# Copying maxima in fewer steps, and preparing the first feed-forward tile beside the end of attention

## What is computed

```
xn  = layernorm(x) * gamma + beta
q, k, v = split(xn @ w_qkv.T)                 # 16 heads of 16
att = softmax(causal(q k^T / 4)) v
x1  = layernorm(x + att)                      # no scale, no shift
h   = silu(x1 w1 * s1) * (x1 w2 * s2)         # 256 -> 1024
h   = gelu(h h1 * s1h); h = gelu(h h2 * s2h)  # 1024 -> 1024, twice
out = layernorm(x1 + h w3 * s3)
```

## Time and profile before

| | us |
|---|---|
| median of 3 launches | 2369.13 (2368.23 to 2370.77) |
| profiled launch, its time | 2370.69 |
| profiled launch, first to last instruction (span) | 2369.0 |
| mean granted TensorE clock, share of 2.4 GHz | 0.987 |

### The profile page before, as it was taken

One profiled execution on the slowest core, in us unless ns is written; L12 is line 12 of the kernel. 1 busy time (PEld: TensorE's weight loads), 2 busy tenths in 40 slices (PEclk: granted clock), 3 DMA queues, 4 the chain that ended last, 5 costly groups with the idle time before them and its releaser, 6 DMA issues. The chain is left out here.

```text
span 2369.0 us, 40425 instructions
## 1 busy us (share of the span) xinstructions
PE 2313.3 (98%) x15360; PEld 1402.8 (59%) x15360; DVE 1737.8 (73%) x3745; ACT 1634.4 (69%) x3221; POOL 204.5 (9%) x266
## 2 busy tenths in 40 slices
PE   5999999999999999999999999999899999999998
PEld 3555554555555455555555555554488888888887
DVE  6889988888889897888879888996335545544543
ACT  2677887788999887888988898999623323332332
POOL 2211100111000101100010211001000000000000
PEclk7999999999999999999999999999899999999999
DMA  4100001100000110000020000205400000000000
GB/s 120 33 23 14 19 19 36 39 19 19 19 11 10 48 28 19 19 19 19 1 50 23 19 19 19 72 2 196 145 1 10 1 9 10 10 1 9 10 1 19
DMA packets 40533, 68.60 MB, mean 29 GB/s; under 512 B 9872, under 2 KB 19984, under 8 KB 38928
## 3 DMA queue, kind: packets, MB, share of 16 engines
q1 hardware_dynamic: 36672, 54.45, 8.4%
q0 software_dynamic: 3664, 11.53, 1.5%
HBM read 28.20 MB, written 4.19 MB: 14 GB/s over the span
## 5 line engine op out<-in xcount | busy, mean ns | idle before, releaser
L620 ACT ACTIVATE PR<-bank 128x512 f32<-128x512 f32 (+3 forms) x2304 | 1110.7, 574 | 61.3 <-PE bank L869 59.1
L696 DVE TENSOR_REDUCE pm<-bank 128x1 f32<-128x512 f32 x1397 | 901.6, 682 | 160.8 <-PE bank L844 145.0
L883 PE MATMUL bank<-PR,V 128*17 128x512 f32 (+3 forms) x4608 | 561.1, 564 | 1.9 <-ACT PR L620 1.2
L1231 PE MATMUL bank<-e_hid,e_h_sb 128*128 128x512 f32 x2048 | 478.1, 395 | 0.0
L864 PE MATMUL bank<-MR,ones 64*128 64x512 f32 (+3 forms) x2304 | 463.4, 390 | 2.2 <-ACT MR L611 0.7
L1231 PEld LDWEIGHTS bank<-e_hid,e_h_sb 128*128 128x128 f32 x2048 | 384.8, 188 | 92.0
L1049 ACT ACTIVATE e_tmp<-bank,e_s_sb 128x512 f32<-128x512 f32 x128 | 88.3, 690 | 342.1 <-PE bank L1231 341.8
L691 DVE TENSOR_REDUCE pm<-mx_sb 128x1 f32<-128x512 f32 x395 | 267.6, 678 | 30.4 <-ACT mx_sb L605 30.3
L864 PEld LDWEIGHTS bank<-MR,ones 64*128 64x128 f32 x2304 | 235.1, 185 | 80.5 <-ACT PR L620 28.9
L605 ACT ACTIVATE mx_sb<-bank 128x512 f32<-128x512 f32 x395 | 238.4, 603 | 45.6 <-PE bank L844 42.1
L699 DVE CUSTOM_DVE_ANT_0 bank<-bank,below 128x384 f32<-128x384 f32 (+3 forms) x512 | 235.7, 520 | 21.3 <-PE bank L844 20.1
(11 more groups left out here) (102 smaller groups left out, 1721.9 us busy)
## 6 DMA issues: line engine op xcount, KB each, us to landing
xnT<-in_h_dram SPq DMA_DIRECT2D x8, 1024.0 KB, 5.7
e_h_sb<-in_h_dram POOLq DMA_DIRECT2D x2, 4096.0 KB, 21.1
KA<-qk_hi SPq DMA_DIRECT2D x96, 64.0 KB, 2.2
KA<-qk_lo SPq DMA_DIRECT2D x96, 64.0 KB, 2.2
QX<-qk_hi SPq DMA_DIRECT2D x80, 64.0 KB, 2.3
QX<-qk_lo SPq DMA_DIRECT2D x80, 64.0 KB, 2.3
xres<-in_x_dram SPq DMA_DIRECT2D x8, 512.0 KB, 8.2
out_dram<-e_y SPq DMA_DIRECT2D x7, 512.0 KB, 2.9
```

Source lines behind the costliest of these rows:

```text
L620: act.activation(PR[:, s % NPB, h, off:QB], ring_bank("score", s, h)[:, off:QB], ACT.Exp).then_inc(exp_done, 1)
L696: dve.reduce_max(pm[:, B % 2, i, a, p, 1 + c:2 + c], bank[:, :], AX.X).then_inc(mx_done, 1)
L883: last = pe.matmul(ACC[32 * h:32 * h + VW, off:QB], V[:, v_tile(B, t), GH * (B // NJ % 2) + h, :], PR[:, s % NPB, h, off:QB], start=(t == ...
L1231: last = pe.matmul(RING[(4 + n) % NR][:, :], w[:, c, P * o:P * (o + 1)], hid[:, (T + layer) % 2, part, c, :], start=(c == 0 and part == 0) ...
```

## The change

In the planner, a relay is no longer placed where one of "norm", "qk", "v", "maxT", "acc" or "acc_copy" stands between "av" and the unit. By the list of operations that takes 79 relays out of 395 and adds none: 23 in steps with "acc_copy", 23 with "acc", 22 with "qk", 3 with "qk" and "acc", 4 with "v", 3 with "norm" and 1 with "norm" and "maxT". `take_banks` then gives other ring banks to the same list.

The preparation of tile T = 0 moves from `feed_forward_exact` into `attend`, under new operations: the statistics on DVE behind "test", the square root on ACT behind the last exponents and ahead of the last "av", the reciprocal and normalisation (into `xn`) on DVE beside it, and after "out" the 8 transposes, the copies and the subtractions. The semaphores of the stage count from T = 1 on. What stays at the stage's start is the in-place normalisation of `xres`, on DVE.

```diff
@@ constants and Schedule @@
+COPIED = ("norm", "qk", "v", "maxT", "acc", "acc_copy")
...
             if (B, t) == (NB - 1, 4):
-                self.ops.append(("test",))
-        self.ops += [("av", len(STEPS) - 2), ("av", len(STEPS) - 1), ("acc_copy", NB - 1), ("acc", NB - 1),
-                     ("out", NB - 1)]
+                self.ops += [("test",), ("x1_stat",)]
+        self.ops += [("x1_std",), ("av", len(STEPS) - 2), ("av", len(STEPS) - 1), ("acc_copy", NB - 1),
+                     ("acc", NB - 1), ("out", NB - 1), ("x1_turn",)]
...
         for op in self.ops:
-            if op[0] == "score":
+            if op[0] == "score" or op[0] in COPIED:
                 after = False
             if op[0] == "av":
                 after = True
...
-            if op[0] == "norm":
+            if op[0] in ("norm", "x1_turn"):
                 for f in range(EC):
-                    n = take(("norm", op[1], f))
+                    n = take(op + (f,))
@@ attend: ACT @@
+            def std_x1():
+                act.wait_ge(x1_stat, 2 * TI)
+                act.activation(std[:, 0, :, :], x1_mean[:, :, 1:2], ACT.Sqrt, bias=eps[:, :]).then_inc(x1_std, 1)
+
+            def copy_x1T():
+                for f in range(EC):
+                    act.wait_ge(x1t_ready, f + 1)
+                    act.activation(x1T[:, 0, f, :], ring_bank("x1_turn", f)[:, :], ACT.Copy).then_inc(x1t_hi, 1)
@@ attend: DVE @@
+            def x1_statistics():
+                dve.wait_ge(res_done, NB - NJ + 1)
+                for i in range(TI):
+                    dve.bn_stats(stats[:, i, :], xres[:, i, :]).then_inc(x1_stat, 1)
+                dve.wait_ge(x1_stat, TI)
+                for i in range(TI):
+                    dve.bn_aggr(x1_mean[:, i, :], stats[:, i, :]).then_inc(x1_stat, 1)
+
+            def x1_normalise():
+                dve.wait_ge(x1_std, 1)
+                dve.reciprocal(x1_rstd[:, :, :], std[:, 0, :, :]).then_inc(x1_inverse, 1)
+                dve.wait_ge(x1_inverse, 1)
+                for i in range(TI):
+                    dve.tensor_scalar(xn[:, i, :], xres[:, i, :], x1_mean[:, i, 0:1], x1_rstd[:, i, :],
+                                      ALU.subtract, ALU.mult).then_inc(x1_done, 1)
+
+            def x1T_low():
+                for f in range(EC):
+                    dve.wait_ge(x1t_hi, f + 1)
+                    dve.tensor_tensor(x1T[:, 1, f, :], ring_bank("x1_turn", f)[:, :], x1T[:, 0, f, :].bitcast(fp32),
+                                      ALU.subtract).then_inc(x1t_lo, 1)
@@ attend: PE @@
+            def transpose_x1():
+                pe.wait_ge(x1_done, TI)
+                for f in range(EC):
+                    ring_free("x1_turn", f)
+                    for i in range(TI):
+                        last = pe.transpose(ring_bank("x1_turn", f)[:, P * i:P * (i + 1)],
+                                            xn[:, i, P * f:P * (f + 1)], ident[:, :])
+                    last.then_inc(x1t_ready, 1)
@@ feed_forward_exact: ACT @@
-                std_x1(0)
-                copy_x1T(0)
                 act.wait_ge(s_load, 16 * 5)
@@ feed_forward_exact: DVE @@
-                x1_statistics(0)
-                x1_normalise(0)
-                x1T_low(0)
+                for i in range(TI):
+                    own = tokens(0)[i]
+                    dve.tensor_scalar(own, own, x1_mean[:, i, 0:1], x1_rstd0[:, i, :], ALU.subtract, ALU.mult)\
+                       .then_inc(x1_kept, 1)
                 dve.wait_ge(s_load, 16 * 5)
@@ feed_forward_exact: PE @@
-                transpose_x1(0)
                 for loaded in early_load:
                     pe.wait_ge(loaded, 16)
...
-                                if o == 0 and at == 0:
-                                    pe.wait_ge(x1t_lo, EC * T + c + 1)
+                                if T > 0 and o == 0 and at == 0:
+                                    pe.wait_ge(x1t_lo, EC * (T - 1) + c + 1)
```

More of the change, by code:

```diff
@@ L282, in block_kernel @@
         low_bits = sb("low_bits", [1, 1], int32)
+        x1_mean = sb("x1_mean", [P, TI, 2])
+        x1_rstd = sb("x1_rstd", [P, TI, 1])
         banks = [ctx.enter_context(nc.psum_tensor(f"bank{i}", [P, 512], fp32)) for i in range(8)]
         attend(nc, x, gamma, beta, wqk, wv, xres, ident, eps, KB, QX, banks, (w1, w2, h1w, h2w, w3), low_bits,
-               tuple(zip(early, (w1, w2, w3), early_load)))
+               tuple(zip(early, (w1, w2, w3), early_load)), x1T, x1_mean, x1_rstd)
         inexact = nc.values_load(low_bits[0:1, 0:1], min_val=0, max_val=2 ** LOW_BITS - 1)
@@ L289, in block_kernel @@
             feed_forward_exact(nc, w1, s1, w2, s2, h1w, h1s, h2w, h2s, w3, s3, out, xres, ident, eps, banks,
-                               x1T, early, early_load)
+                               x1T, early, early_load, x1_mean, x1_rstd)
         with nc.Else():
@@ L300, in clear, with attend @@
     nc.all_engine_barrier()
-def attend(nc, x, gamma, beta, wqk, wv, xres, ident, eps, KB, QX, banks, ff_weights, low_bits, early):
+def attend(nc, x, gamma, beta, wqk, wv, xres, ident, eps, KB, QX, banks, ff_weights, low_bits, early, x1T, x1_mean,
+           x1_rstd):
     with ExitStack() as ctx:
@@ L388, in attend @@
         first_chunk = sem("first_chunk")
+        x1_stat = sem("x1_stat")
+        x1_std = sem("x1_std")
+        x1_inverse = sem("x1_inverse")
+        x1_done = sem("x1_done")
+        x1t_ready = sem("x1t_ready")
+        x1t_hi = sem("x1t_hi")
+        x1t_lo = sem("x1t_lo")
         chunk_load = [sem(f"chunk_load{i}") for i in range(2)]
@@ L656, in _ @@
                     copy_sums(op[1])
+                if op[0] == "x1_std":
+                    std_x1()
+                if op[0] == "x1_turn":
+                    copy_x1T()
         @block.vector
@@ L774, in _ @@
                     test_weights()
+                if op[0] == "x1_stat":
+                    x1_statistics()
+                if op[0] == "x1_std":
+                    x1_normalise()
+                if op[0] == "x1_turn":
+                    x1T_low()
         @block.tensor
@@ L914, in _ @@
                     transpose_acc(op[1])
+                if op[0] == "x1_turn":
+                    transpose_x1()
 def feed_forward_exact(nc, w1, s1, w2, s2, h1w, h1s, h2w, h2s, w3, s3, out, xres, ident, eps, banks,
-                       x1T, early, early_load):
+                       x1T, early, early_load, x1_mean, x1_rstd0):
     with ExitStack() as ctx:
@@ L1008, in std_x1 @@
                 def std_x1(T):
-                    act.wait_ge(x1_stat, NS * (T + 1))
+                    act.wait_ge(x1_stat, NS * T)
                     act.activation(std[:, :, :], mv[:, :, 1:2], ACT.Sqrt, bias=eps[:, :]).then_inc(x1_std, 1)
@@ L1021, in copy_x1T @@
                     for f in range(EC):
-                        act.wait_ge(x1t_ready, EC * T + f + 1)
+                        act.wait_ge(x1t_ready, EC * (T - 1) + f + 1)
                         act.activation(x1T[:, 0, f, :], TB[f][:, :], ACT.Copy).then_inc(x1t_hi, 1)
@@ L1068, in x1_statistics @@
                         dve.bn_stats(stats[:, i, :], tokens(T)[i]).then_inc(x1_stat, 1)
-                    dve.wait_ge(x1_stat, NS * T + TI)
+                    dve.wait_ge(x1_stat, NS * (T - 1) + TI)
                     for i in range(TI):
@@ L1073, in x1_normalise @@
                 def x1_normalise(T):
-                    dve.wait_ge(x1_std, T + 1)
+                    dve.wait_ge(x1_std, T)
                     if T >= 2:
@@ L1078, in x1_normalise @@
                     dve.reciprocal(rstd[:, :, :], std[:, :, :]).then_inc(x1_rstd, 1)
-                    dve.wait_ge(x1_rstd, T + 1)
+                    dve.wait_ge(x1_rstd, T)
                     for i in range(TI):
@@ L1089, in x1T_low @@
                     for f in range(EC):
-                        dve.wait_ge(x1t_hi, EC * T + f + 1)
+                        dve.wait_ge(x1t_hi, EC * (T - 1) + f + 1)
                         dve.tensor_tensor(x1T[:, 1, f, :], TB[f][:, :], x1T[:, 0, f, :].bitcast(fp32), ALU.subtract)\
@@ L1191, in transpose_x1 @@
                 def transpose_x1(T):
-                    pe.wait_ge(x1_done, TI * (T + 1))
+                    pe.wait_ge(x1_done, TI * T)
                     for f in range(EC):
```

## The result

| | before | after |
|---|---|---|
| median, launches side by side (us) | 2369.95 (4) | 2354.82 (4) |
| ratio, 95% interval | | 0.9934 (0.9917 to 0.9951) |
| profiled launch, its time (us) | 2370.69 | 2352.26 |
| mean granted clock | 0.987 | 0.990 |

15.1 us less were measured, 17.2 were predicted. The profiled launch of after is the fastest of its four, 2.6 us under their median, so its rows show more gain than the median does. They split the time in three. The last exponents end at 1666.60 instead of 1683.92: 17.3 us won in attention. From there to the end of the first tile's 64 matmuls it is 1.1 us longer. The rest of the feed-forward part is 2.5 us shorter, which the prediction did not have.

A forecast was written before the change was run, and what follows sets the result against it. PE was taken to set the pace mid-block, relays costing time only where ACT has further copies. First edit -19.5 and second +2.3 make -17.2, so 2369.1 becomes 2352 us; own range 2340 to 2364 (chance 0.62), stated range 2340 to 2366.

The forecast's parts named there:

- First edit: Attention steps with further ACT copies: 79 relays fewer save 19.5 us, extremes 1.7 and 33 us less.
- "acc_copy": 23 steps with the accumulator's copy: 0.27 us less each, 6.2 us in all, from blocks 17 and 11.
- "qk" and "norm": 25 projection steps and 4 first-norm steps, two copies on ACT: 0.4 us less each, 10.0 and 1.6 us.
- "v": 4 steps at a block's end: 7.23 us with a relay, 6.80 without, so 0.43 each, 1.7 us less.
- "acc": 23 steps where ACT waits for PE and the relay lies in its slack: nothing, bounds 0.27 either way.
- "A relay changes nothing": Middle of a block: PE sets the 2.59 us pace without a hole, so a relay there is worth nothing.
- Second edit: Seam to feed-forward, first tile prepared early: costs 2.3 us, 1.3 at the stage's start and 1.0 in the first tile.
- scales land early: Rival, first feed-forward tile: product of chunk 0 ready by about 7, PE never stands, 6.4 us won, 2344.5 us; chance 0.10.
- The table change: Attention's end, ACT's square root: table load of 1.28 us alone counted; the skill's extra drain would add an estimated 1.4 us.
- Given back: Rival: next steps wait as long for banks or PE, 0 to 3 us won, 2.3 lost, about 2369; chance 0.14.
- full relief: Rival: ACT sets the pace through block starts, each relay worth 0.48 us, 38 us in all, 2333 us; chance 0.08.
- Slower: Rival: banks return some 0.6 us later through DVE and PE stops; 24 us more, 2395 us; chance 0.06.

The follow-up runs named there:

- e5: Kernel before, with relays taken out only of the 23 steps with the copy of the accumulator: 8.3 us less than before, ratio 0.9965.
- e6: Kernel before, with relays taken out only of the 29 steps with the projection's or first norm's copies: 9.0 us less than before, ratio 0.9962.
- e8: Kernel before, with all 395 relays taken out: 26.2 us more than before, ratio 1.0112.
- e2: Changed kernel with all 395 relays kept, so only the early preparation of the first tile is new: 2371.53 us, ratio 1.0007 to before.
- e9: Changed kernel with the scale vectors allocated ahead of the hidden layers' weights in SBUF, same instructions: 2342.24 us, ratio 0.9887 to before.
- e4: Changed kernel with POOL waiting for the five scale vectors before issuing the hidden layers' weights: 2348.78 us, ratio 0.9912 to before.
- e1: Kernel before with only the 79 relays taken out, first tile prepared where it was: 2353.72 us, ratio 0.9931 to before.

## Why the prediction was right

By its own steps:

- **First edit, -19.5 predicted, -16.4 measured**, with -19.7 to -13.0 as the interval. (Its extreme of 33 us less comes to 2369.1 - 33 + 2.3 = 2338.4, where the text has 2340; the result lies far from either.) Direction and mechanism held: the relay held ACT where ACT had further copies, and the steps are shorter by it. "acc_copy" was taken at 0.27 a step; e5 has 8.3 / 23 = 0.36, with an interval from 0.22 to 0.49, and 0.25 in the rows of block 17. "qk" and "norm" were taken at 0.4; e6 has 9.0 / 29 = 0.31, from 0.20 to 0.42, and the rows of block 10 have 0.41. So neither size is refuted. "v" was a term of 1.7 that isn't there in the trace; it came from comparing block 20 with block 3, and in block 20 itself the stretch went from 7.23 to 7.19 us. "acc", taken at nothing, is at +1.5 with nothing in its interval.
- **"A relay changes nothing" in a plain step** is the claim that fell. A PE that shows no hole at 2.59 us a step was read as a PE that sets the pace whatever the relay does. e8 shows that the step is 2.69 without it. The change leaves the 316 alone, so the error cost the forecast nothing.
- **Second edit, +2.3 predicted, +1.4 measured**, with nothing inside the interval. e2 also has the 1.6 us that the last layer wins by its addresses, so the seam by itself is nearer +3.0. The rows differ from launch to launch: from the last exponents to the end of the first tile's 64 matmuls it is 1.1 us longer than before in after, 4.1 in e2 and 3.8 in e9. Both terms vary:
  - The stage's start was predicted 1.3 later. It is 7.39 us behind the last exponents in after, 7.85 in e2, 8.12 in e9 and 8.11 in e4, and 6.73 before: 0.7 to 1.4 later. The eight transposes ran at full clock in after, 1.09 us, and took 1.72 us in e2 and 1.97 in e9 and e4.
  - The first tile's end, counted from the stage's start, was predicted 1.0 later. It is 0.4 later in after, 2.9 in e2 and 2.4 in e9. PE was to restart at 13.2. The silu's table load, which the prediction had put behind the landing of the scales, ran while ACT was still waiting for them (1677.85, wait of the activation behind it), and so PE restarts at 11.7 in after; in e2 and e9 the scales landed later and it is 14.2. The slow clock cost 11.90 - 9.2 = 2.7 us at the restart, not 2.0.
- **Luck in the sum.** The first edit gave 3.1 us less than forecast and the second cost 0.9 less, so the sum is off by 2.2 only. But the 0.9 comes out of the last layer's 1.6 us, which was not foreseen at all and has nothing to do with either edit's mechanism.
- **The scales.** The rival "scales land early" fell with the 8.3 us of its row. Its way there, DVE's in-place normalisation beside POOL's issue, is in the rows of after: DVE from 1674.02 for 1.75 us, POOL from 1674.43 for 1.82. POOL's issue took 1.81 us before and wasn't held up. It was DVE that lost: 1.75 us for four instructions, which take 1.38 before and in e4, where POOL isn't issuing beside them. By its rule in the Trainium skill ("SBUF — State Buffer", section "SBUF: two separate sides") POOL's issue would starve while DVE holds the port pair that they share; here that did not show. The prediction's "No row of before shows that overlap" holds for this instruction alone: DVE's statistics (L1068, 1690.68 to 1692.09) ran beside POOL's issue, which began at 1691.08. e4 shows what does hold the scales: the weights' traffic.
- **The table change.** The root starts at 1667.90, right behind a load of 1.28 us from 1666.61. The extra drain that the Trainium skill states ("ScalarE: Activation LUTs", section "What ACT_TABLE_LOAD costs"), by which the sum would have been an estimated 1.4 us longer, isn't in these rows.
- "Given back" would have won 3 us at most and "full relief" 38; e1 has 16.4. "Slower" had banks returning late through DVE. A cost of that sort exists, as e8 shows with 0.13 us a relay, but not in the 79 steps that the rule picks.

What remains open is which wait costs the plain step its 0.1 us without the relay, and why SP's issues and the landing of the scales are longer in e2 and e9 than in after.

## What to carry to other kernels

A copy that relieves one engine is worth what it returns to the engine that waits, and that is different in every kind of step: price it by taking it out in one kind at a time. Work moved ahead of a stage only wins what the next input allows; here PE started 6 us sooner and then waited for small vectors beside 8 MB of weights, which cost 6.5 us and could be had by issuing them during the stage before. One profiled launch can be a lucky one: after's seam was 3 us shorter than that of two other kernels with the same seam. Any edit that allocates memory moves what lies behind it, so a time that changes in untouched matmuls is to be checked against the addresses before it is put down to the edit.

## What the runs showed of the hardware

- A stream of matmuls with weight loads ran at two paces by the places of its two operands in SBUF alone: 256 in 58.1 us (227 ns each) with 65536 bytes from `h1_sb` to `hid`, and in 59.5 to 59.7 (232 to 233 ns) with 66688; 64 of the last layer in 7.67 or 7.47 us for a shift of `hid` by 64 bytes.
- A 128 KB broadcast issued by SP landed after 3.2 us alone (e4), and beside 8 MB of POOL's after 8.3 (before, after) or 9.7 (e2, e9).
- Four DVE instructions of 128x256 took 1.75 us beside POOL's issue (after) and 1.38 without it (e4).
- The clock fell at different idle times of PE. After its stop at 1681.4 in after it stayed 1.00 until 1684 and was 0.64 in the microsecond from there. Before, with transposes until 1686.6, it was 0.79 in the microsecond from 1687. The restarts cost 2.7 and 2.0 us against full clock.
- A table load does not wait for what its activation waits for: it ran at 1677.85, the activation at 1684.11.
